# Factors of the negated maxima and variance sums read from a column of constants, and a maximum of two halves folded by a tensor_reduce

## The reference

```python
def _layernorm(x, axis=-1, eps=1e-05):
    m = jnp.mean(x, axis=axis, keepdims=True)
    v = jnp.var(x, axis=axis, keepdims=True)
    return (x - m) / jnp.sqrt(v + eps)

# self attention
scores = jnp.einsum('bhqd,bhkd->bhqk', q, k) * scale
scores = jnp.where(causal[None, None], scores, jnp.float32(-jnp.inf))
attn = jax.nn.softmax(scores, axis=-1)
out = jnp.einsum('bhqk,bhkd->bhqd', attn, v)
...
x = _layernorm(x + attention(x), axis=-1)
x = _layernorm(x + cross_attention(x, ctx), axis=-1)
x = _layernorm(x + experts(x), axis=-1)
```

## Time and profile before

| | us |
|---|---|
| median of three timed runs | 687.06 |
| lowest and highest of them | 686.52, 689.18 |
| the profiled execution | 685.79 |
| its span (first to last instruction) | 683.8 |
| VectorE busy | 516.5 |
| TensorE busy | 601.9 |
| GpSimd busy | 294.1 |
| mean granted clock of TensorE | 0.972 |

### The profile page before, as it was taken

One profiled execution on the slowest core, in us unless ns is written; L12 is line 12 of the kernel. 1 busy time (PEld: TensorE's weight loads), 2 busy tenths in 40 slices (PEclk: granted clock), 3 DMA queues, 4 the chain that ended last, 5 costly groups with the idle time before them and its releaser, 6 DMA issues.

```text
span 683.8 us, 22315 instructions
## 1 busy us (share of the span) xinstructions
PE 601.9 (88%) x8065; PEld 444.5 (65%) x8065; DVE 516.5 (76%) x1110; ACT 397.7 (58%) x846; POOL 294.1 (43%) x246
## 2 busy tenths in 40 slices
PE   2689889999999999989897688789999999999990
PEld 1357656666667776757565465667878888888860
DVE  5887998898775878767677987676776666666655
ACT  5335678857567567567767867445444444444434
POOL 4778583633455724453201111233444444444433
PEclk9989999999999999999999999899999999999995
DMA  8445353050241211422526004411232232222534
GB/s 277 160 110 141 94 149 116 18 168 4 77 114 56 63 41 59 118 60 76 144 78 195 24 32 151 136 32 33 36 52 49 49 56 48 48 49 48 125 70 138
DMA packets 39924, 59.75 MB, mean 87 GB/s; under 512 B 6832, under 2 KB 27568, under 8 KB 39696
## 3 DMA queue, kind: packets, MB, share of 16 engines
q1 hardware_dynamic: 32336, 48.12, 23.8%
q0 software_dynamic: 7488, 10.23, 9.1%
HBM read 34.08 MB, written 11.67 MB: 67 GB/s over the span
## 4 chain that ended last, share of the span: by engine, by line
PE 43%; DVE 9%; ACT 3%; DMA 2%; issue 2%; SPq 1%; POOL 0%; ACTq 0%; DVEq 0%; POOLq 0%
PE bank L1734 9%; PE bank L1736 4%; PE scores L1724 3%; DVE mxc L1110 3%; PE scores L1726 3%; PE scores L1725 3%; PE bank L1724 2%; PE bank L1726 2%; PE bank L1725 2%; PE bank L1361 2%; PE bank L1335 2%; PE scores L1386 1%; PE scores L1461 1%; ACT probs L767 1%; PE scores L1431 1%
## 5 line engine op out<-in xcount | busy, mean ns | idle before, releaser
L767 ACT ACTIVATE probs<-scores 128x768 f32<-128x768 f32 (+1 forms) x128 | 114.4, 918 | 53.6 <-PE scores L1392 40.9
L652 POOL DMA_INDIRECT acc_rows<-x,slot_row x39 | 63.8, 1636 | 118.7 <-DVE x L1242 112.0
L1734 PE MATMUL bank<-w_sb,wp 128*128 x312 | 109.8, 379 | 2.2 <-DVE wp L1229 2.2
L1110 DVE TENSOR_REDUCE mxc<-scores 128x4 f32<-128x1024 f32 x64 | 76.5, 1218 | 20.2 <-PE scores L1406 19.8
L1736 PE MATMUL bank<-w_sb,wp 128*128 x312 | 85.1, 273 | 0.0
L838 ACT ACTIVATE probs<-scores,b_sb 128x128 f32<-128x128 f32 x160 | 45.5, 369 | 60.9 <-PE scores L1726 60.9
L838 ACT ACTIVATE probs<-bank,b_sb 128x128 f32<-128x128 f32 x152 | 43.5, 369 | 57.4 <-PE bank L1726 57.3
L1227 DVE CAST wp<-probs 128x512 f16<-128x512 f32 x78 | 34.4, 441 | 55.2 <-ACT probs L838 54.7
L1075 DVE TENSOR_REDUCE mx<-scores 128x6 f32<-128x768 f32 x64 | 59.8, 951 | 14.0 <-PE scores L1374 13.7
L1724 PE MATMUL scores<-xT,w_sb 128*128 128x128 f16 x320 | 60.6, 222 | 2.5 <-DVE xT L931 1.5
L614 POOL TENSOR_TENSOR w_sb<-w_sb 128x512 f16<-128x512 f32 x32 | 37.6, 1181 | 55.8 <-ACT w_sb L740 55.6
(11 more groups left out here) (275 smaller groups left out, 1716.8 us busy)
## 6 DMA issues: line engine op xcount, KB each, us to landing
w_sb<-w_sb SPq DMA_DIRECT2D x192, 64.0 KB, 2.3
wstage<-in_w_exp SPq DMA_DIRECT2D x16, 512.0 KB, 4.3
w_sb<-in_w_exp SPq DMA_DIRECT2D x8, 512.0 KB, 5.6
wp<-in_w_exp SPq DMA_DIRECT2D x8, 512.0 KB, 4.1
x_sb<-in_x_by_feature SPq DMA_DIRECT2D x8, 256.0 KB, 3.6
ctx_raw<-in_ctx SPq DMA_DIRECT2D x8, 256.0 KB, 3.0
x_res<-in_x SPq DMA_DIRECT2D x8, 256.0 KB, 3.2
x_rows<-x SPq DMA_DIRECT2D x8, 256.0 KB, 2.9
```

The lines of the kernel that those rows point to most:

```text
L652: nc.gpsimd.indirect_dma_start(out=acc_rows[:, :], out_offset=bass.IndirectOffsetOnAxis(ap=slot_row[:, n:n + 1], axis=0), in_=yb[n % 2], i ...
L767: nc.scalar.activation(probs[:, 2 * (k % 4):2 * (k % 4) + 2, 0:cols], ps_p[pair[u, k, b]][:, :, 0:cols], ACT.Exp, scale=(SELF_SCALE, CROSS ...
L1110: nc.vector.tensor_reduce(mxc[:, 2 * k:2 * k + 2, :], ps_p[pair[u, k, b]][:, :, :].rearrange("p h (a k) -> p h a k", a=2), axis=AX.X, op=A ...
L1734: mm(o[:, 0:2 * D], ah[:, u, f, :], weights(e, at, 2 * D), start=(f == 0), stop=(f == FC - 1), skip_group_check=True)
```

## The change

The table gets two more columns, `C_MINUS` with -1.0 and `C_EPS` with the epsilon of the layer norm. The two negations of `self_negate`, the two of `cross_negate` and the sum at the end of `layer_norm` name such a column, one number for each partition, in the place of the number in the instruction. The maximum of `mx[:, :, 1]` and `mx[:, :, 2]` is taken by a tensor_reduce over the last axis of `mx[:, :, 1:3]`, in the place of a tensor_tensor. That is five lines, and over all batches 48 instructions with a column and 8 folds. The lists of units, the semaphores and the number of instructions stay as they were.

```diff
-C_ALL = C_BEFORE + E
+C_MINUS = C_BEFORE + E
+C_EPS = C_MINUS + 1
+C_ALL = C_EPS + 1
...
-                nc.vector.tensor_scalar(rstd[a][:, :], mv[a][:, :, 1], LN_EPS, None, ALU.add).then_inc(v_var[a], 1)
+                nc.vector.tensor_scalar(rstd[a][:, :], mv[a][:, :, 1], tab[:, C_EPS:C_EPS + 1], None, ALU.add).then_inc(v_var[a], 1)
...
                 elif u == "self_negate":
                     dve.wait_ge(v_max[0], b * (H // 2) + H // 2)
                     nm = negm[0][:, :, :].rearrange("p t (a n) -> p t a n", a=2)[:, :, :, 0:H // 2]
-                    nc.vector.tensor_scalar(nm[:, 0], mx[:, :, 0].rearrange("p (n a) -> p a n", a=2), -1.0, None, ALU.mult)
-                    link(nc.vector.tensor_tensor(mx2[:, :], mx[:, :, 1], mx[:, :, 2], ALU.max))
-                    nc.vector.tensor_scalar(nm[:, 1], mx2[:, :].rearrange("p (n a) -> p a n", a=2), -1.0, None,
+                    minus = tab[:, C_MINUS:C_MINUS + 1]
+                    nc.vector.tensor_scalar(nm[:, 0], mx[:, :, 0].rearrange("p (n a) -> p a n", a=2), minus, None, ALU.mult)
+                    link(nc.vector.tensor_reduce(mx2[:, :], mx[:, :, 1:3], axis=AX.X, op=ALU.max))
+                    nc.vector.tensor_scalar(nm[:, 1], mx2[:, :].rearrange("p (n a) -> p a n", a=2), minus, None,
                                             ALU.mult).then_inc(v_nm[0], 1)
...
                     for t in range(TT):
-                        last = nc.vector.tensor_scalar(nm[:, t], mxc[:, :, t].rearrange("p (n a) -> p a n", a=2), -1.0,
-                                                       None, ALU.mult)
+                        last = nc.vector.tensor_scalar(nm[:, t], mxc[:, :, t].rearrange("p (n a) -> p a n", a=2),
+                                                       tab[:, C_MINUS:C_MINUS + 1], None, ALU.mult)
...
+    t[:, C_MINUS], t[:, C_EPS] = -1.0, LN_EPS
```

## The result

| | kernel before | changed kernel |
|---|---|---|
| median of the timed runs (18 each, us) | 688.07 | 690.63 |
| ratio to the kernel before, with its 95% interval | | 1.0042 (1.0025 to 1.0059) |
| the profiled execution (us) | 685.79 | 689.80 |
| its span (us) | 683.8 | 687.6 |

The changed kernel is slower, by 0.42% or 2.9 us (1.7 to 4.1; the two medians differ by 2.6). That is under the 0.5% that I called visible, and well above the 1.1 us that I forecast.

What follows compares the result with a forecast made beforehand. TensorE and VectorE, both nearly full before 432 us, set the end by turns; 1.61 us x 0.45 plus 1.34 x 0.30 gave +1.1 us on the 687.06 median, 688.2 us, range 684.6 to 690.8 (the forecast's own 687.1 to 690.0).

Steps and rivals of the forecast that it cites:

- The price of a column: In the negations and variance sums: a column in place of a number adds 59 ns of VectorE to each instruction.
- those that stand: Negations and variance sums starting within a GpSimd instruction wait until it ends, 6.7 us in all; columns would not stop this.
- the fold is worth nothing: Eight folds of self maxima: tensor_reduce costs 15 ns more each, 0.12 us of VectorE, with no waits for GpSimd to save.
- The first rival: Columns free the negations and sums from waiting for GpSimd: all 6.7 us go, -1.6 us on the path, 685.5; chance 0.22.
- the mean of the eight L1086, 170 ns, shows no such meeting: Fold of the self maxima: the tensor_tensor never waits for GpSimd, so replacing it gives nothing back.
- 8 bytes more on a row of the table: Load of the constants at the start: two more columns lengthen it by under 0.1%, costing 0.
- I cost the change of the standing at 0.: Waits of negations and sums behind GpSimd stay as they are: 0, with ends of -6.7 and some +3 us.
- the second rival: Self groups and sums between 60 and 150 us meet GpSimd more often: 2.7 us more, 690.9; chance 0.13.
- The shares 0.45 and 0.30: Part of each added VectorE microsecond that reaches the end: 0.45 before 255 us, 0.30 behind it.
- 48 columns: 32 negations and 16 variance sums, each 0.059 us longer: 2.83 us of VectorE.
- at most 62/177 = 35%: Between 255 and 432 us: VectorE's 62 us in the chain of waits taken as the upper limit of its share.

Runs made afterwards that it cites:

- free_all: Kernel before, with negations as tensor_reduce with negate flag (folding second self maxima) and epsilon as a third column added by tensor_reduce: 0.9998 (0.9976 to 1.0021).
- eps_only: Kernel before, with the column in the 16 variance sums alone: 1.0017 (0.9996 to 1.0037).
- delay runs: Kernel before, with idle VectorE reduces ahead of the places of the change, before 255 us in one run (1.0067, +4.6 us), behind it in the other (1.0039, +2.7 us).
- batch3_numbers: Changed kernel, with numbers in place of columns in the two cross negations of batch 3: 1.0012 (0.9994 to 1.0031) against the kernel before.
- delay_late: Kernel before, with an idle VectorE reduce ahead of each of 15 places of the change behind 255 us: 1.0039 (1.0021 to 1.0058), +2.7 us.

## Why the prediction was off

**Right.** The price of a column (59 ns; measured 228 against 168 and, for a second one, 288), that a column keeps the instruction among those that stand (durations of 1108, 967 and 1177 ns), that the fold is worth nothing, that all of it happens before 432 us, and that the change ends within 0.5% on the slow side. The first rival, freed instructions, is out. The Trainium skill ("SBUF — State Buffer", section Who interferes with whom) says that a VectorE instruction in a two-port mode, which a tensor_scalar can enter, and a GpSimd instruction exclude each other, and that tensor_reduce never contends. The trace agrees: tensor_scalar with a column stood for up to 1177 ns, and none of the 48 reduces of `free_all` took over 193.

Two readings were wrong without bearing on the sum. That "the mean of the eight L1086, 170 ns, shows no such meeting" hides that two of the eight started 3 and 8 ns ahead of GpSimd's, a near miss of the fold, which came true once, in `eps_only`. And 8 bytes more on a row of the table are 0.2% of its load, not under 0.1%.

**Wrong by its size.** 2.9 us where I had 1.1. The steps that failed:

1. *"I cost the change of the standing at 0."* One new standing of 0.96 us came, and it costs 1.0 to 1.2 us in the start of what follows, by four traces. It is the second rival's mechanism at another place and a smaller price: I looked for it at the self groups and the sums between 60 and 150 us, and set the cross negations aside because none had met GpSimd. That they had not met it says nothing. The timeline had GpSimd starting 0.05 us behind the second one, and I added 0.06 us ahead of it.
2. *The shares 0.45 and 0.30.* Added work at these places reached the end at 0.74 and 0.51 in the delay runs (0.9 and 0.7 of what VectorE lost net). `batch3_numbers` has 27 columns between 114 and 326 us, of which 8 are on instructions that stand; the other 19 give VectorE 1.12 us, and its row rises by 0.78, a share of 0.7. VectorE's busy time in that stretch is up by 0.79 us only, in part because those that stand are 0.19 us shorter together, so of its busy time nearly all arrives. The share isn't the same throughout: between 239.6 and 285.1 us the row rises by 0.22 for 0.19 us of busy time, between 285.1 and 325.7 by 0.04 for 0.31. The chain of waits names one engine at each moment, and an engine that it doesn't name may lack only tens of nanoseconds; I took its share as the most that could arrive ("at most 62/177 = 35%"), and the runs went above it.
3. *48 columns.* Twelve or so are read while the instruction stands and cost nothing, so 36 x 0.059 = 2.1 us in place of 2.83. This went the other way.

Put together: 2.1 x 0.7 + 1.1 = 2.6 us, in the interval of 1.7 to 4.1. The rest isn't settled; the gap of TensorE at 192 us is one candidate.

And the same share was used for the gain in the first rival (-1.6). `free_all` shows that it isn't the same: 7.6 us less of VectorE gave 0.

## What to carry to other kernels

Before a change that lengthens or shortens instructions by tens of nanoseconds, look in the timeline of the kernel before for what starts within that distance of them, above all where one engine stands behind another: a near miss can cost the whole of the other's instruction, and within some 10 ns the timeline doesn't tell which way it falls. Loss and gain of the same microsecond of a nearly full engine can have different shares: here half or more of the added time arrived at the end, while the removed time went in the next waits. And where the times can't tell, pair the same instructions of two traces and read the steps, with the stretches in which both run the same instructions as the measure of the noise.

## What the runs showed of the hardware

Which of VectorE and GpSimd stands depends on when each starts, and one execution can differ from the next in it. The instructions up to 255 us are the same in the kernel before and in `delay_late`, yet at 109 us the one has VectorE stand and the other GpSimd. Kernel before, VectorE and then GpSimd:

```profile
109.50 2.18 DVE L1081 SCALAR_TENSOR_TENSOR w_sb<-w_sb 128x1024 f16<-128x1024 f32 x1
...
108.93 1.67 POOL L614 TENSOR_TENSOR w_sb<-w_sb 128x512 f16<-128x512 f32 x1 [8.74 <-ACT w_sb L740]
```

The same two in `delay_late`:

```profile
109.72 1.22 DVE L1084 SCALAR_TENSOR_TENSOR w_sb<-w_sb 128x1024 f16<-128x1024 f32 x1
...
109.94 2.02 POOL L615 TENSOR_TENSOR w_sb<-w_sb 128x512 f16<-128x512 f32 x1 [8.78 <-ACT w_sb L741]
```

GpSimd came 0.6 us ahead of VectorE in the first and 0.2 us behind in the second, 1.0 us later than in the first. VectorE's instruction is 0.96 us shorter in the second and GpSimd's 0.35 us longer, and the row of `delay_late` falls by 1.7 us around it. So part of the spread of the kernel before (685.35 to 690.39 us in 18 runs) may be of this kind; no trace of its other runs shows it.

Not every GpSimd instruction holds VectorE. In the kernel before, the two scalings L899 at 163.43 and 163.75 us start within the root L586 of 2 elements (163.28 to 163.98) and take their usual 404 and 408 ns.

A tensor_reduce with the negate flag over an axis of one element is a negation that takes 172 to 175 ns, about as much as an undisturbed tensor_scalar (168), and none of the 24 in `free_all` stood behind GpSimd, though four of them started within one of its instructions.
